# Routed FFN behind graph attention: four banks for each engine in the node loop, root node ahead of the sort, final stores that add to an output that holds x

## The chip, the cores and the metric

One core of one Trainium2 chip runs the whole program. The metric is the device time of one execution in microseconds. The core's engines are TensorE (PE, matrix products into PSUM), VectorE (DVE), ScalarE (ACT), GpSimd (POOL) and SyncE (SP, which here only issues DMAs). The kernel uses PSUM as eight banks of 128 partitions by 512 f32 values.

## The reference

```python
x = x + gnn(layernorm(x), neigh, adj, ...)        # x: 512 x 128, adj: 512 x 512, 8 heads
h = layernorm(x)
current = 0                                       # each token starts at the root of a tree, 255 nodes
for level in range(8):
    score = h . w1s[current] + b1s[current]
    out  += gelu(|score|) * (h @ w2s[current] + b2s[current])
    current = 2 * current + 1 + (score > 0)
return x + out
```

Every token goes down a binary tree. At each of its eight nodes it is multiplied by that node's own 128 x 128 matrix. Node 0, the root, is on the path of every token.

## The kernel before

The first part (up to about 61 us) is the attention: scores, softmax and weighted values for 4 tiles of 128 tokens and 8 heads. Then x1 = x + attention is made (512 x 128, in `x1`), normalised, turned (`h_t`), and scored against all 255 nodes at once. DVE makes `path`, a 0/1 row of nodes per token. The tokens are then sorted by their leaf: a permutation matrix `perm` sorts, on PE, the paths (L745 into `s_ps`), the weights (L745 into `aux_ps`) and the tokens themselves (L784, `hs_t` after ACT's copy L522). In a sorted tile of 128 tokens only few nodes occur. They are written out as one list per tile, `nodes` (PE L791, ACT L524), made up to a multiple of 8 entries with a node that has coefficient 0. `coef` holds, for each sorted token and node, gelu(|score|) or 0 (DVE L1094), and its transpose `coef_t` serves for the biases b2 (PE L563, ACT L531).

The node loop is what runs last. Every turn takes 8 list entries of one sorted tile. PE multiplies the tile's tokens by the eight node matrices (L820), product j into bank j: `s_ps` holds banks 0 to 3, `turn_ps` 4 and 5, `aux_ps` 6, `misc_ps` 7. DVE takes banks 0, 2, 3, 5, 7: it multiplies by the node's column of `coef` and adds to one of three sums in `acc` (an early name of that room is `early`, and so it stands in the profile), all in one instruction (L1115). ACT takes banks 1, 4, 6: it scales into `scaled_sb` (L542), and POOL adds that to one of two more sums (L401). A bank is free for the next turn when its consumer is done (`emptied`). All four engines run the same loop (`tile_turns`, a hardware loop per tile with a turn count from the list's length), and each has to read the list entries into registers: PE eight at the head of a turn (L97), DVE and ACT eight in the middle of it (L85). L90 is the address worked out from such a register, L118 the loop.

After a tile's turns PE makes the bias products (L830) and ACT moves them (L549). DVE sums the six partial sums of a tile in one reduction (L1130), for tiles 0 and 1 after tile 1, for tile 2 after tile 2, for tile 3 at the end. x1 itself comes in by a detour: it is written in token order to `x1_rows` in HBM (ACT L491), gathered from there by the sorted token numbers into the first sum (POOL L384), and the summed tile is scattered to the output by the same numbers (POOL L409).

The reference's inputs give the four sorted tiles 31, 24, 17 and 48 nodes that occur, root included, and so 4, 3, 3 and 6 turns, 16 together.

## Time and profile before

| | us |
|---|---|
| median of 3 runs | 137.24 |
| lowest, highest | 135.8, 138.54 |
| the profiled execution | 134.76 |
| its span in the profile | 133.0 |
| busy PE / DVE / ACT / POOL | 107.4 / 96.7 / 66.0 / 38.7 |
| TensorE's granted clock, mean of the span | 0.985 of full |

The span runs from the first to the last instruction of the trace, and the profiled execution's own time is 1.76 us more. The sections of the profile used here are the chain that ended last, the groups of instructions by line, and the timeline, in which every row is an instruction or a run of like ones, with its start, its length, its engine and line, what it writes and reads, and in brackets how long the engine sat idle before it and for whom.

### The profile page before, as it was taken

The numbers are of one execution on the slowest core, as the hardware profiler recorded it, in microseconds if no ns is written. First come the engines' busy times: TensorE is split into PE (matmuls) and PEld (weight loads), VectorE is DVE, ScalarE is ACT, GpSimd is POOL, SyncE is SP. The second block draws the span as 40 slices with busy tenths as digits, with TensorE's granted clock in tenths as the row PEclk, the third lists the DMA queues.
The fourth block names the chain that finished last, engine by engine and source line by source line (L and its number), as shares of the span: only waits on it lengthen the run. The fifth ranks groups of instructions, "written<-read, shape, count | busy, mean of one in ns | idle before, by whom it ended". The sixth has DMA issues, their size and how long they took to land.

```text
span 133.0 us, 3457 instructions
## 1 busy us (share of the span) xinstructions
PE 107.4 (81%) x984; PEld 76.2 (57%) x985; DVE 96.7 (73%) x293; ACT 66.0 (50%) x149; POOL 38.7 (29%) x84
## 2 busy tenths in 40 slices
PE   6989889559999999988998679989888499678800
PEld 2349663335656566657564353788778388578700
DVE  1787799988989989825888995367455976856760
ACT  3047288549777967931191644634344233344300
POOL 6394000000000000000400023155566436855552
PEclk9999999999999999999999999999999999999995
DMA  3998899989992000029992001000000000100000
GB/s 96 324 312 273 374 463 473 424 362 463 463 419 103 2 0 5 0 68 378 386 412 82 1 0 44 0 0 0 20 2 0 22 0 2 39 0 0 0 20 20
DMA packets 3420, 20.14 MB, mean 151 GB/s; under 512 B 465, under 2 KB 2000, under 8 KB 2896
## 3 DMA queue, kind: packets, MB, share of 16 engines
q1 hardware_dynamic: 2048, 18.42, 34.2%
q10 hardware_dynamic: 1104, 1.05, 2.5%
q0 software_dynamic: 256, 0.52, 1.4%
q8 instruction: 6, 0.10, 0.3%
q14 instruction: 6, 0.05, 0.1%
HBM read 19.47 MB, written 0.52 MB: 150 GB/s over the span
## 4 chain that ended last, share of the span: by engine, by line
PE 33%; DVE 19%; issue 10%; DVEq 10%; ACT 7%; POOL 1%
PE turn_ps L674 9%; DVE early L1115 6%; DVEq L90 4%; PE s_ps L820 4%; DVEq L85 4%; PE s_ps L620 3%; ACT prob L474 3%; DVE x L1130 2%; PE misc_ps L639 2%; DVE token_path L1034 2%; PE turn_ps L820 1%; PE s_ps L707 1%; PE s_ps L559 1%; PE turn_ps L563 1%; ACT prob_t L470 1%
## 5 line engine op out<-in xcount | busy, mean ns | idle before, releaser
L401 POOL TENSOR_TENSOR early<-early,scaled_sb 128x128 f32<-128x128 f32 x48 | 21.1, 455 | 20.0 <-ACT scaled_sb L542 18.4
L820 PE MATMUL s_ps<-w,msg 128*128 x128 | 18.8, 287 | 7.5 <-issue 3.6
L474 ACT ACTIVATE prob<-prob,negmax 128x512 f32<-128x512 f32 x32 | 21.7, 715 | 6.1 <-DVE negmax L994 6.1
L994 DVE CUSTOM_DVE_ANT_0 prob<-s_ps,mask 128x512 f32<-128x512 f32 x32 | 21.0, 685 | 3.3 <-PE s_ps L620 2.6
L674 PE MATMUL turn_ps<-ident,prob 128*128 128x128 f32 x128 | 19.2, 283 | 3.7 <-ACT prob L474 3.7
L820 PEld LDWEIGHTS s_ps<-w,msg 128*128 128x128 f32 x128 | 15.6, 191 | 10.5 <-issue 10.3
L1115 DVE SCALAR_TENSOR_TENSOR early<-s_ps,coef,early 128x128 f32<-128x128 f32 x48 | 14.2, 346 | 7.6 <-PE s_ps L820 4.3
L674 PEld LDWEIGHTS turn_ps<-ident,prob 128*128 128x128 f32 x128 | 13.6, 141 | 10.5 <-ACT prob L474 10.1
L373 POOL TENSOR_TENSOR rstd<-veps,mhalf 128x2 f32<-128x2 f32 x2 | 1.4, 714 | 52.4 <-DVE veps L854 52.4
L542 ACT ACTIVATE scaled_sb<-s_ps,coef 128x128 f32<-128x128 f32 x16 | 5.9, 368 | 14.6 <-PE s_ps L820 13.1
L1115 DVE SCALAR_TENSOR_TENSOR early<-turn_ps,coef,early 128x128 f32<-128x128 f32 x16 | 5.6, 350 | 9.2 <-issue 8.5
L542 ACT ACTIVATE scaled_sb<-turn_ps,coef 128x128 f32<-128x128 f32 x16 | 5.9, 367 | 9.4 <-PE turn_ps L820 9.4
L820 PE MATMUL turn_ps<-w,msg 128*128 x64 | 9.9, 277 | 0.0
L620 PE MATMUL s_ps<-early 32*128 32x512 bf16 x96 | 7.4, 377 | 2.2 <-DVE negmax L994 1.9
L1003 DVE COPY w<-turn_ps 128x512 f32<-128x512 f32 x12 | 8.3, 690 | 0.8 <-PE turn_ps L674 0.7
L470 ACT ACTIVATE w<-turn_ps 128x512 f32<-128x512 f32 x12 | 7.1, 592 | 3.4 <-PE turn_ps L674 2.8
L820 PEld LDWEIGHTS turn_ps<-w,msg 128*128 128x128 f32 x64 | 8.4, 192 | 0.1
L559 PE MATMUL s_ps<-count_row,ones_h 128*128 128x512 f16 x33 | 8.4, 379 | 0.0
L384 POOL DMA_INDIRECT early<-x_rows,token_s x4 | 4.1, 1026 | 14.3 <-ACT token_s L519 13.6
L1130 DVE TENSOR_REDUCE x<-early 128x128 f32<-128x768 f32 x4 | 5.8, 1463 | 1.1 <-DVE early L1115 1.1
L579 PE MATMUL s_ps<-early 128*128 128x512 bf16 x12 | 5.2, 624 | 1.3 <-DVE early L880 1.3
L820 PE MATMUL aux_ps<-w,msg 128*128 x32 | 6.2, 275 | 0.0
(189 smaller groups left out, 196.2 us busy)
## 6 DMA issues: line engine op xcount, KB each, us to landing
w<-in_w_t SPq DMA_DIRECT2D x3, 4096.0 KB, 22.9
w<-in_w_t SPq DMA_DIRECT2D x1, 4032.0 KB, 14.2
w<-in_adj SPq DMA_DIRECT2D x1, 1024.0 KB, 8.4
w_sb<-in_w_t ACTq DMA_DIRECT2D x1, 384.0 KB, 4.4
x_sb<-in_x SPq DMA_DIRECT2D x1, 256.0 KB, 3.2
msg<-in_neigh_t SPq DMA_DIRECT2D x1, 256.0 KB, 4.0
x_rows<-x ACTq DMA_DIRECT2D x1, 256.0 KB, 10.2
row_sb<-in_rows ACTq DMA_DIRECT2D x1, 255.5 KB, 7.7
```

The costliest lines, as they stand in the source:

```text
L401: nc.gpsimd.tensor_tensor(mine, mine, scaled_sb[:, i, :], ALU.add).then_inc(pooled[i], STEP)
L470: nc.scalar.activation(slots[v % SLOTS], turn_ps[0][:], ACT.Copy).then_inc(moved[0], 1)
L474: nc.scalar.activation(prob[:, u % RING, :], prob[:, u % RING, :], ACT.Exp, bias=negmax[:, t, h:h + 1], scale=-1.0).then_inc(exped, 1)
L542: nc.scalar.activation(scaled_sb[:, i, :], product_ps[j], ACT.Copy, scale=coef[:, s, bass.ds(node_at(nc.scalar, entry, j), 1)]).then_inc(s ...
L559: nc.tensor.matmul(s_ps[:, 3, :], ones_h[:], count_row[:], start=True, stop=True)
L620: ins = nc.tensor.matmul(score_ps[u % RING], q_st[rows, q, g, t * P:(t + 1) * P], k_st[rows, k, g, :], start=(i == 0), stop=(i == len(PROD ...
L674: last = nc.tensor.transpose(turn_ps[u % 2][:, m * P:(m + 1) * P], prob[:, u % RING, m * P:(m + 1) * P], ident[:])
L820: nc.tensor.matmul(product_ps[j], hs_t[:, s * P:(s + 1) * P], w2_flat[:, bass.ds(found[j], D)], start=True, stop=True).then_inc(multiplied ...
L994: nc.vector.tensor_tensor_reduce(out=prob[:, u % RING, :], in0=score_ps[u % RING], in1=mask[:, t, :], scale=1.0, scalar=0.5 * MASKED, op0= ...
L1003: nc.vector.tensor_copy(slots[v % SLOTS], turn_ps[1][:]).then_inc(moved[1], 1)
L1115: nc.vector.scalar_tensor_tensor(out=mine, in0=product_ps[j], scalar=coef[:, s, bass.ds(node_at(nc.vector, entry, j), 1)], in1=mine, op0=A ...
L1130: nc.vector.tensor_reduce(result[:, tile, :], acc[:, :, tile, :].rearrange("p j d -> p d j"), AX_X, ALU.add).then_inc(tile_done, 1)
```

## The change

- **Banks.** DVE takes banks 1, 3, 5, 7 with two sums and ACT takes banks 0, 2, 4, 6. POOL adds two scaled products in one instruction of 128 x 256, two such a turn in place of three of 128 x 128. DVE and ACT read only their own four entries, at the head of a turn.
- **Root.** It is left out of the sort's lists. Behind the node scores PE multiplies `h_t` by the root's matrix, unsorted, and ACT scales it (`root_sb`). The lists then hold 30, 23, 16 and 47 nodes, and so 4, 3, 2 and 6 turns.
- **Output.** `x1_rows`, its store and the four gathers go. POOL adds `root_sb` to `x1`, SP stores that to `out` in token order, and each sorted tile is then added to `out` by a scatter whose DMA adds.
- **Sums.** The reductions L1130 go. After tiles 0, 1 and 2 POOL itself adds up four sums in two instructions (three for tile 0, which has its bias apart), and issues the scatter. Only the last tile's are added by DVE.
- **First turn.** The first turn stands ahead of the loop and ahead of the transposes of `coef`. The list is made in two halves, and the sorting of the tokens in two halves around that of the weights. Nine fillers (`keep_busy`) stand where 13 did, and the four ahead of the loop go.

On PE, between the sort of the paths and the node loop, the instructions stood in this order (`w` is the node matrices, `msg` the sorted tokens, `prob` the permutation and the chosen lists):

```order
L745 MATMUL s_ps<-token_path,prob 128x256 x15
L745 MATMUL aux_ps<-picked_p,prob 128x24 [waits counts_moved,picked_split]
L784 MATMUL turn_ps<-prob,h_p 128x512 x7
L791 MATMUL s_ps<-prob,node_col 1x512 [waits chosen_ready]
L791 MATMUL s_ps<-prob,node_col 1x512 x3
L559 MATMUL s_ps<-count_row,ones_h 128x512 [waits path_s_ready]
L105 TENSOR_LOAD entries [waits w2_in3,b2_in,w2_in2,lengths_ready,w2_in1,w2_in0]
L563 MATMUL turn_ps<-ident,coef 128x128 [waits coef_ready,hs_ready,lists_ready]
L563 MATMUL misc_ps<-ident,coef 128x128 x4
L97 TENSOR_LOAD row_room
L820 MATMUL s_ps<-w,msg 128x128
```

and stand now in this one:

```order
L810 MATMUL s_ps<-token_path,prob 128x256 x15
L844 MATMUL s_ps<-prob,node_col 1x512 [waits chosen_ready]
L853 MATMUL turn_ps<-prob,h_p 128x512 x3
L810 MATMUL aux_ps<-picked_p,prob 128x24 [waits counts_moved,picked_split]
L853 MATMUL turn_ps<-prob,h_p 128x512 x4
L844 MATMUL s_ps<-prob,node_col 1x512 [waits chosen_ready]
L98 TENSOR_LOAD row_room [waits lists_ready,weights_added,path_s_ready]
L890 ISA [waits scaled0,hs_ready]
L890 MATMUL s_ps<-w,msg 128x128
L890 MATMUL misc_ps<-w,msg 128x128
L617 MATMUL s_ps<-ident,coef 128x128 [waits scaled0,coef_ready]
L617 MATMUL s_ps<-ident,coef 128x128 [waits scaled1]
```

The first eight node products no longer wait for `coef`, and its transposes stand behind them. Half of the list and half of the sorted tokens come ahead of the weights' sort.

On POOL one tile's loop and what follows it was, for the first tile (the scatters came later):

```order
L401 TENSOR_TENSOR early<-early,scaled_sb 128x128 [waits pooled2,scaled0]
L401 TENSOR_TENSOR early<-early,scaled_sb 128x128 [waits scaled1]
L401 TENSOR_TENSOR early<-early,scaled_sb 128x128 [waits pooled0,scaled2]
L118 COMPARE_AND_BRANCH
L384 DMA early<-x_rows,token_s 128x128
```

and is now:

```order
L419 TENSOR_TENSOR early<-early,scaled_sb 128x2x128 [waits scaled1,pooled1,scaled0]
L419 TENSOR_TENSOR early<-early,scaled_sb 128x2x128 [waits scaled3,pooled0,scaled2]
L123 REGISTER_ALU x3
L123 COMPARE_AND_BRANCH
L425 REGISTER_ALU x2
L429 TENSOR_TENSOR early<-early 128x2x128 [waits added3,added2,pooled1]
L433 TENSOR_TENSOR x<-early 128x128 [waits x1_out,result_ready]
L439 TENSOR_TENSOR x<-x,early 128x128 [waits bias_moved,result_ready]
L444 DMA out_x<-x,token_s 512x128 [waits tile_done]
```

Each add of a pair waits for the one before it, and the tile's own sums stand in POOL's queue ahead of the next tile's adds.

On DVE one turn, from the loop's head to its end, was

```order
L90 ISA [waits added3,multiplied0]
L1115 SCALAR_TENSOR_TENSOR early<-s_ps,coef,early 128x128
L90 ISA [waits added4,multiplied2]
L90 ISA [waits multiplied3]
L85 TENSOR_LOAD row_room
L1113 REGISTER_ALU [waits multiplied5]
L1115 SCALAR_TENSOR_TENSOR early<-turn_ps,coef,early 128x128
L90 ISA [waits added1,multiplied7]
L1115 SCALAR_TENSOR_TENSOR early<-misc_ps,coef,early 128x128
L118 COMPARE_AND_BRANCH
```

and is now

```order
L123 ISA
L85 TENSOR_LOAD row_room
L90 ISA [waits added2,multiplied1]
L1193 SCALAR_TENSOR_TENSOR early<-s_ps,coef,early 128x128
L90 ISA [waits added3,multiplied3]
L1191 REGISTER_ALU [waits multiplied5]
L1193 SCALAR_TENSOR_TENSOR early<-turn_ps,coef,early 128x128
L90 ISA [waits added1,multiplied7]
L1193 SCALAR_TENSOR_TENSOR early<-misc_ps,coef,early 128x128
L123 REGISTER_ALU x3
L123 COMPARE_AND_BRANCH
```

One instruction on a bank is gone, the load of the entries moved from the middle to the head, and three register operations stand at the loop's end. The core of the diff:

```diff
-DVE_BANKS = (0, 2, 3, 5, 7)
-ACT_BANKS = (1, 4, 6)
-DVE_SUMS = 3
+HALVES = 1
+TURN = HALVES * STEP
+DVE_BANKS = (1, 3, 5, 7)
+ACT_BANKS = (0, 2, 4, 6)
+DVE_SUMS = 2
...
     start = STEP
+    whole_turn(0, STEP, 0)
+    begun()
     for s in range(TILES):
...
+        with eng.Fori(start + TURN if s == 0 else start, end, TURN) as e:
+            whole_turn(s, e, e - start + s * NODES_PAD)
         after(s, end)
...
+            sp.wait_ge(root_added, 1)
+            sp.dma_start(out.rearrange("(t p) d -> p t d", p=P), x1[:]).then_inc(x1_out, 16)
...
+            pool.wait_ge(coef_ready, 2)
+            nc.gpsimd.tensor_tensor(x1[:], x1[:], root_sb[:], ALU.add).then_inc(root_added, 1)
+
+            def add_scaled(s, half, e, at):
+                for i in range(len(pooled)):
+                    pool.wait_ge(scaled[2 * i], e + STEP)
+                    pool.wait_ge(scaled[2 * i + 1], e + STEP)
+                    pool.wait_ge(pooled[1 - i], e + (HALVES - 1 + i) * STEP)
+                    mine = acc[:, DVE_SUMS:SUMS, s, :]
+                    slot = half * len(ACT_BANKS) + 2 * i
+                    nc.gpsimd.tensor_tensor(mine, mine, scaled_sb[:, slot:slot + 2, :], ALU.add
+                                            ).then_inc(pooled[i], STEP)
...
+                nc.gpsimd.indirect_dma_start(out=out, out_offset=bass.IndirectOffsetOnAxis(
+                    ap=token_s[:, s:s + 1], axis=0), in_=result[:, s, :], in_offset=None, compute_op=ALU.add
+                                             ).then_inc(stored, 16)
...
+            for t in range(TILES):
+                nc.scalar.activation(root_sb[:, t, :], turn_ps[1][:, t * P:(t + 1) * P], ACT.Copy,
+                                     scale=root_w[:, t:t + 1]).then_inc(root_scaled, 1)
...
-            keep_busy(13)
+            for t in range(TILES):
+                nc.tensor.matmul(misc_ps[:, t:t + 1], ones_row[:], row_sb[0:1, B1:B1 + 1], start=True, stop=False)
+                last = nc.tensor.matmul(misc_ps[:, t:t + 1], h_t[:, t * P:(t + 1) * P], w1_sb[:, 0:1],
+                                        start=False, stop=True)
+            last.then_inc(root_scored, 1)
+            pe.wait_ge(w2_in[0], 16)
+            for t in range(TILES):
+                last = nc.tensor.matmul(turn_ps[1][:, t * P:(t + 1) * P], h_t[:, t * P:(t + 1) * P], w2[:, 0, :],
+                                        start=True, stop=True)
+            last.then_inc(root_scored, 1)
+
+
+            keep_busy(9)
...
             def sum_up(s, end):
+                if s == TILES - 1:
+                    for i in range(DVE_SUMS, len(DVE_BANKS)):
+                        dve.wait_ge(added[i], end)
+                    dve.wait_ge(pooled[1], end + (HALVES - 1) * STEP)
+                    mine = acc[:, 0:DVE_SUMS, s, :]
+                    then(nc.vector.tensor_tensor(mine, mine, acc[:, DVE_SUMS:SUMS, s, :], ALU.add))
+                    nc.vector.tensor_tensor(result[:, s, :], acc[:, 0, s, :], acc[:, 1, s, :], ALU.add
+                                            ).then_inc(tile_done, 1)
```

## Rows read from the trace of the kernel before

**Rows 1.** Chain that ended last, one piece of tile 3 (start us, us, what).

```profile
118.99 0.35 DVEq L85
```

**Rows 2.** Timeline, two turns of tile 3: DVE alone.

```profile
117.18 0.35 DVE L1115 SCALAR_TENSOR_TENSOR early<-turn_ps,coef,early 128x128 f32<-128x128 f32 x1 [0.66 <-issue]
...
118.11 0.88 DVE L1115 SCALAR_TENSOR_TENSOR early<-s_ps,coef,early 128x128 f32<-128x128 f32 x3 [0.31 <-issue]
119.65 0.35 DVE L1115 SCALAR_TENSOR_TENSOR early<-turn_ps,coef,early 128x128 f32<-128x128 f32 x1 [0.66 <-issue]
```

**Rows 3.** Timeline, third and fourth turn of tile 0: PE, ACT, POOL.

```profile
88.95 1.15 PE L820 MATMUL s_ps<-w,msg 128*128 x8 [0.25 <-issue]
...
89.82 0.37 ACT L542 ACTIVATE scaled_sb<-s_ps,coef 128x128 f32<-128x128 f32 x1 [0.79 <-PE s_ps L820]
...
90.32 0.46 POOL L401 TENSOR_TENSOR early<-early,scaled_sb 128x128 f32<-128x128 f32 x1 [0.54 <-ACT scaled_sb L542]
...
90.96 0.36 ACT L542 ACTIVATE scaled_sb<-aux_ps,coef 128x128 f32<-128x128 f32 x1
...
91.15 1.15 PE L820 MATMUL s_ps<-w,msg 128*128 x8 [0.15 <-issue]
```

**Rows 4.** Timeline: what stands between tiles, and the end.

```profile
93.03 1.06 PE L830 MATMUL s_ps<-b_sb,prob_t 128*128 128x128 f32 x8
...
103.15 2.86 DVE L1130 TENSOR_REDUCE x<-early 128x128 f32<-128x768 f32 x2 [0.63 <-DVE early L1115]
...
115.97 0.45 POOL L401 TENSOR_TENSOR early<-early,scaled_sb 128x128 f32<-128x128 f32 x1 [0.17 <-POOL early L401]
...
127.91 1.45 DVE L1130 TENSOR_REDUCE x<-early 128x128 f32<-128x768 f32 x1 [0.24 <-DVE early L1115]
129.63 0.96 POOL L409 DMA_INDIRECT out_x<-x,token_s  x1 [1.02 <-DVE x L1130]
```

**Rows 5.** Timeline ahead of the node loop.

```profile
67.96 2.97 PE L559 MATMUL s_ps<-count_row,ones_h 128*128 128x512 f16 x13
...
71.40 0.25 PE L725 MATMUL aux_ps<-ones_h,token_path 128*128 128x1 f16 x4 [0.47 <-DVE token_path L1034]
...
78.59 0.56 PE L745 MATMUL aux_ps<-picked_p,prob 128*128 128x24 bf16 x16 [0.81 <-DVE picked_p L867]
...
79.01 1.89 PE L784 MATMUL turn_ps<-prob,h_p 128*128 128x512 f16 x8
...
80.11 1.70 DVE L1094 TENSOR_TENSOR coef<-token_path_s,weight_s 128x4 f32<-128x4 f16 x8
...
80.83 1.02 PE L791 MATMUL s_ps<-prob,node_col 128*1 128x512 f16 x4
...
80.93 0.60 ACT L522 ACTIVATE msg<-turn_ps 128x512 f32<-128x512 f32 x1 [2.03 <-PE turn_ps L784]
...
81.89 1.01 ACT L524 ACTIVATE row_room<-s_ps 1x1024 int32<-1x1024 f32 x1 [0.36 <-PE s_ps L791]
...
83.96 1.15 PE L820 MATMUL s_ps<-w,msg 128*128 x8
```

**Rows 6.** Timeline around POOL's one wide add.

```profile
9.58 0.74 DVE L877 SCALAR_TENSOR_TENSOR w<-w,from_even 128x512 f32<-128x512 bf16 x1
9.66 1.80 POOL L368 TENSOR_TENSOR x_sb<-x_sb,row_sb 128x512 f32<-128x512 f32 x1
...
10.97 0.78 DVE L917 TENSOR_TENSOR early<-w,early 128x256 bf16<-128x256 f32 x1 [0.65 <-ACT early L448]
```

**Rows 7.** Groups of instructions by line, whole span, shapes apart.

```profile
L917 DVE TENSOR_TENSOR early<-w,early 128x768 bf16<-128x768 f32 x1 | 0.9, 948 | 0.0
...
L1010 DVE TENSOR_TENSOR x<-x_sb,misc_ps 128x256 f32<-128x256 f32 x1 | 0.4, 422 | 1.3 <-PE misc_ps L702 1.3
```

**Rows 8.** DMA issues, median us from issue to landing.

```profile
early<-x_rows,token_s POOLq DMA_INDIRECT x4, 2.6
out_x<-x,token_s POOLq DMA_INDIRECT x4, 2.2
```

More of the change, by code:

```diff
@@ L105, in list_lengths, with tile_turns, whole_turn, gnn_ffn_kernel @@
     _, lengths = nc.values_load_multi_w_load_instructions(
-        entries[0:1, 0:TILES], engines=(engine,), min_val=STEP, max_val=NODES_PAD)
-    return lengths
-def tile_turns(eng, lengths, entry, nodes, turn, after):
+        entries[0:1, 0:TILES], engines=(engine,), min_val=TURN, max_val=NODES_PAD,
+        skip_runtime_bounds_check_because="lengths are counts of nodes turned up to at least one turn")
+    return lengths
+def tile_turns(eng, lengths, turn, begun, after):
+    def whole_turn(s, e, at):
+        for half in range(HALVES):
+            turn(s, half, e + half * STEP, at + half * STEP)
     start = STEP
+    whole_turn(0, STEP, 0)
+    begun()
     for s in range(TILES):
-        end = eng.snap(lengths[s] + start)
-        if entry is not None:
-            first_entries(eng, entry, nodes, s)
-        with eng.Fori(start, end, STEP) as e:
-            turn(s, e, e - start + s * NODES_PAD)
+        end = eng.snap((lengths[s] & (2 * NODES_PAD - TURN)) + start)
+        with eng.Fori(start + TURN if s == 0 else start, end, TURN) as e:
+            whole_turn(s, e, e - start + s * NODES_PAD)
         after(s, end)
         start = end
-def gnn_ffn_kernel(nc, x, adj, neigh_t, w_t, cols, rows, w1_t, w2_t, b2, x1_rows, out):
+def gnn_ffn_kernel(nc, x, adj, neigh_t, w_t, cols, rows, w1_t, w2_t, b2, out):
     with ExitStack() as ctx:
@@ L403, in store @@
-            def store(s, end):
-                if s < GROUPS[0][1]:
-                    gather(s + GROUPS[0][1])
-                for tile in STORED_AFTER[s]:
-                    pool.wait_ge(tile_done, tile + 1)
-                    nc.gpsimd.indirect_dma_start(out=out, out_offset=bass.IndirectOffsetOnAxis(
-                        ap=token_s[:, tile:tile + 1], axis=0), in_=result[:, tile, :], in_offset=None
-                                                 ).then_inc(stored, 16)
-            tile_turns(nc.gpsimd, list_lengths(nc, pool.engine, entries), None, nodes, add_scaled, store)
+            pool.wait_ge(acc_zero, SUMS)
@@ L772, in _, with lists, sorted_h @@
             last.then_inc(path_sorted, 1)
+            def lists(half):
+                pe.wait_ge(chosen_ready, 2 * (half + 1))
+                for c in range(2):
+                    last = nc.tensor.matmul(s_ps[0:1, half, :], node_col[:, c:c + 1],
+                                            chosen[:, c, half * 512:(half + 1) * 512],
+                                            start=(c == 0), stop=(c == 1))
+                last.then_inc(listed, 1)
+            def sorted_h(t0, t1):
+                for t in range(t0, t1):
+                    for i in range(2):
+                        last = nc.tensor.matmul(turn_ps[1][:], h_p[:, t, i, :], perm[:, t, :],
+                                                start=(t == 0 and i == 0), stop=(t == TILES - 1 and i == 1))
+                return last
+            lists(0)
+            pe.wait_ge(h_split, 2)
+            sorted_h(*GROUPS[0])
             pe.wait_ge(picked_split, 2 * PARTS - 1)
@@ L802, in _, with products @@
             lengths = list_lengths(nc, pe.engine, entries)
-            pe.wait_ge(lists_ready, 1)
-            pe.wait_ge(hs_ready, 1)
-            pe.wait_ge(coef_ready, 1)
-            for c in range(2):
-                transposes((turn_ps[1], misc_ps)[c], coef[:, :, c * P:(c + 1) * P], coef_turned)
+            pe.wait_ge(path_s_ready, 1)
+            pe.wait_ge(weights_added, 1)
+            pe.wait_ge(lists_ready, 2)
             w2_flat = w2[:].rearrange("p n o -> p (n o)")
-            def products(s, e, at):
+            def products(s, half, e, at):
```

275 lines of the change are left out of this document (147 added, 128 removed).

## Prediction

> **What bounds the kernel now.** Read the chain that ended last first, since a mean of busy time hides where the end is set. From 95 us on it runs over DVE: its adds L1115, its register load L85 [rows 1] and its reductions L1130. The timeline of DVE alone shows why. A turn takes 119.65 - 117.18 = 2.47 us [rows 2]: three adds 0.27 apart (0.88 in all), 0.66 idle while eight entries are loaded, two adds, and 0.31 idle at the loop's end. Add up to see that nothing else is in it: 0.88 + 0.66 + 0.62 + 0.31 = 2.47. PE alone is faster: in tile 0, where it runs ahead, its turns are 91.15 - 88.95 = 2.20 us apart [rows 3]. So DVE sets the pace of the loop, and between tiles it stops for the reductions, 2.86 + 1.45 us inside the loop and 1.45 at the end [rows 4]. The node loop begins at 83.96 [rows 5] and the last sum is ready at 127.91 + 1.45 = 129.36, which leaves 133.0 - 129.36 = 3.64 us for the scatter.
>
> **The change, part by part.** I place each turn by the start of its first product, T1 to T15, and build a new timeline in the time of the profiled span (133.0).
>
> *Root ahead of the sort.* PE runs 13 fillers in 2.97 us and then sits idle 0.47 for the path [rows 5]. Four fillers go (4 x 0.214 = 0.86). New are four products of 128 x 128 in f32, eight passes of 0.11 as in the loop (16 passes in about 1.76) = 0.88, and eight of one column, 16 passes. Those are not in the trace. Below they cost 0.035 each (the 16 narrow ones of the weights' sort, 0.56), above 0.11 each (1.76). I take 0.06, nearer the narrow rows, since one column streams nothing and only the f32 load is left: 0.96. Net 0.88 + 0.96 - 0.86 = 0.98, less the 0.47 of idle: PE is 0.5 late, with ends 0.1 and 1.3. As the fillers may overlap a little with that I take **+0.4**, and everything behind moves by it, since DVE waits there for PE's count. ACT's new work (two small, four of 128 x 128) fits its idle time before it needs the scores.
>
> *First turn sooner.* PE waited 0.81 for the weights' split at 78.59 [rows 5]. Half of the list (half of 1.02) and half of the tokens (half of 1.89) now fill that. The sort of the paths frees PE at about 77.6, so the order ends at 77.6 + 0.47 + 0.92 + 0.56 + 0.92 + 0.47 = 80.95. ACT copies the tokens (0.60) from 80.7 and then the list's second half (0.55 of 1.01), to 81.9, where it ended at 82.90. With the register load of some 0.45, T1 = 82.4 against 83.96. `coef` (until 81.81) no longer bounds PE. DVE's and ACT's first instructions wait for it and for their loads until about 83.0, when the first product is just out. The eight transposes (0.9) follow the first turn: T2 = 82.4 + 1.78 + 0.9 + 0.42 = 85.5, against 86.65 before. Cover gone would show as T2 later by ACT's two copies of 0.60.
>
> *Banks.* DVE's turn is now 3 x 0.27 + 0.35 = 1.16 of adds, plus 0.66 and 0.31 if load and loop end stand one behind the other: 2.13, and some 0.1 for three register operations. ACT's is the same. PE needs 2.20 and gets the same register operations. I take **2.25** a turn for all three, PE being the bound by a hair. One turn of 16 is gone. T3 to T15 are 13 x 2.25, and two bias blocks of 0.9 [rows 4] stand between: without further waits T15 = 85.5 + 29.25 + 1.8 = 116.55.
>
> *POOL.* The new question is its add of 128 x 256. The 128 x 128 one takes 0.46 [rows 3], the only wide one, 128 x 512, took 1.80 [rows 6]. A straight line through both gives 0.90. But that wide one started under a DVE instruction with two SBUF inputs that ended at 10.32, and the DVE instruction after it, again with two SBUF inputs, took 0.78 us for 256 columns [rows 6], where the same form with 768 took 0.95 [rows 7]: each held the other up. Taken from 10.32, POOL's ran 1.14 us, a slope of 1.8 ns a column, and 128 x 256 costs 0.46 + 128 x 0.0018 = 0.69. DVE's adds in the loop have one SBUF input (the other is PSUM), and POOL's 0.46 there does not waver. I take 0.70. The Trainium skill, "SBUF — State Buffer", section "Who interferes with whom", says the same as a rule: a DVE instruction with two SBUF inputs contends with a GpSimd one that reads SBUF, and the later one waits. By that rule 0.70 stands and the forecast is 130.7. By the plain line of the rows (0.90) it would be 134.6, as the rival below works out.
>
> A turn on POOL is then 2 x 0.70 + 0.17 (the wait for its own last add over the loop's end [rows 4]) + 0.05 for the same wait inside the turn, a guess that no row bounds from above but the 0.17, = 1.62 < 2.25. Behind a tile stand its sums and the scatter: 0.70 + 2 x 0.46 + 0.96 [rows 3, 4] and some 0.6 of waits between them (0.17 each) = 3.2 for tile 0, 2.7 for tiles 1 and 2 with one add less. ACT's last scaling starts 2.0 after T (90.96 - 88.95), so a turn's pairs end at T + 2.0 + 0.37 + 0.13 + 0.70 = T + 3.2 and start at T + 1.6. A first pair that is late by L frees ACT's room at T + 2.3 + L and PE's bank at T + 2.85 + L, which PE wants two turns on, at T + 4.5: L up to 1.65 costs nothing. After tile 0, L = 3.2 + 3.2 - (2.25 + 0.9 + 1.6) = 1.65. Each turn after a tile's first wins back 2.25 - 1.62 = 0.63, so tile 1 ends with L = 0.4, and tile 2 begins with 3.2 + 0.4 + 2.7 - 4.75 = 1.55. Tile 2 has two turns and no bias block: L = 3.2 + 0.9 + 2.7 - (2.25 + 1.6) = 2.95, which is 1.3 over the 1.65 that is free, a stall of **1.3**. T15 = 117.85, and POOL's last add ends at 121.1.
>
> *The end.* DVE's two adds (0.42 [rows 7], some 0.3, waits 0.1) replace 0.24 + 1.45: 121.9. Then the same 3.64 as before: 125.5. The scatter now adds. No row shows one. Below it costs nothing more; above, one more trip like the gather's, 2.6 us [rows 8], in place of part of the 2.2. I take **0.5**, since it moves the same 512 bytes a row and only its read of HBM is new. The Trainium skill, "DMA: Bandwidth & Descriptors", section "Rules for kernel authors", states that an accumulating DMA reads its destination and writes it later, and prices neither. That reading in full is a rival below. The store of x1 by SP (after the weights, its queue is empty) starts near 83.5 and is wanted near 94, so it is hidden; late, it would hold POOL at tile 0. The removed gathers and the removed store of x1 were off the path.
>
> Sum: 125.5 + 0.5 + 0.4 = 126.4, and 126.5 unrounded, a gain of 6.5 on 133.0. The profiled execution (134.76) lies below all three runs shown, so I set the gain against their median: 137.24 - 6.5 = **130.7**.
>
> **The rivals.**
> 1. *POOL becomes the bound* (its wide add takes 0.90). Then POOL never rests from tile 0 on. From T4 = 90.0 its last add ends at 90.0 + 3.6 + 3.4 + 2.9 + 2.9 + 11 x 2.02 = 125.0 in place of 121.1: 134.6. For it: the raw row of 1.80. Against: the DVE row of 0.78.
> 2. *The load at the head costs what it cost in the middle, and more*: DVE and ACT take 2.45 a turn. 13 x 0.20 = 2.6: 133.3. For it: load, loop end and register operations now stand in one string with no product to hide behind. Against: the branch back is issued while the last adds run, so that part of the 0.31 falls away.
> 3. *The scatter reads first, a whole trip*: + 2.1, 132.8. For it: the rule named above. Against: only the last scatter is on the path.
> 4. *The other side: the adding scatter is dear on POOL itself.* If its issue takes X more than 0.96, the three inside the loop delay POOL by 3X and the last the end by X. POOL has 121.1 - 119.6 = 1.5 in hand over the whole loop (90.0 + 3.2 + 3.2 + 2.7 + 2.7 + 11 x 1.62 = 119.6), so the end moves by 4X - 1.5. It is slower than before by 2% (140.0) from X = 2.7, and at X = 3, so 4 us a scatter, it gives 141.2. For it: nothing shown. Against: the gather and the plain scatter, both near 1.0.
> 5. *No change within 2%*: rival 1 and the root's upper price (1.3 in place of 0.4) together, 134.6 + 0.9 = 135.5.
>
> **How the numbers follow.** Forecast 0.55, rival 1 0.13, rival 2 0.12, rival 3 0.11, rival 4 0.05, rival 5 0.04. Below, with no stall, no cost of the adding scatter and none of the root, it is 128.5, and 1 us of spread between runs makes 127.5. Above, rivals 1 to 3 lie inside 135.0. Two per cent is about what a measurement of this kernel can tell, that is below 134.5 for faster. Half of rival 1 falls above it, with rival 5 and part of rival 2: faster 0.80, same 0.14, slower 0.06.
>
> **What would show it.** Right: PE's turns 2.2 to 2.3 us apart; L419 on POOL near 0.70 each; first product about 1.2 us sooner; no DVE reduction in the loop; 15 turns; one wait of PE near the second turn of the last tile, traced back to POOL. Wrong: POOL busy without a gap from tile 1 on (rival 1), DVE with over 1.2 us idle a turn on "issue" (rival 2), over 4.5 us from the last DVE add to the end (rival 3), scatters over 2 us on POOL (rival 4). TensorE's clock stays at 9 tenths in the page through the waits at the tiles' ends today, and the new ones are no longer; a fall to the lower level would be an error of mine.

## The result and the profile after

The changed kernel takes 138.32 us (median of 4, 137.76 to 139.5), the kernel before 136.52 beside it on the same chip (135.33 to 138.54): a ratio of 1.022 [1.016, 1.028], so slower by 1.6 to 2.8%. The forecast was 130.7. The profiled span is 136.0 us, against 133.0 before and 126.5 in the sum.

Executions of one and the same kernel differ by how often TensorE's granted clock falls to its lower level: the 23 of the kernel before that stood beside the last experiments run from 134.5 us at a mean granted clock of 0.985 over 136.4 at 0.963 to 138.2 at 0.951, so the ratios here leave out executions over 1.5% above the fastest of their kernel, and I judge the steps of the sum by stretches of the traces whose clock is known.

The first row of clocks is that of the profile after, 40 equal slices of 3.4 us. It falls at 29 to 33 us, in a part that the change does not touch, and again near 105:

```profile
PEclk9999999977999999999999999999998699999985
```

The timeline at the root's products (start us, us, engine, line; PE's work and the first instruction of DVE behind it):

```profile
68.93 0.38 PE L776 MATMUL misc_ps<-row_sb,ones_row 1*128 1x1 f32 x2
69.24 0.38 PE L777 MATMUL misc_ps<-w_sb,h_t 128*128 128x1 f32 x2
...
71.34 1.14 PE L782 MATMUL turn_ps<-w,h_t 128*128 128x128 f32 x8
72.32 2.11 PE L613 MATMUL s_ps<-count_row,ones_h 128*128 128x512 f16 x9
74.26 0.24 PE L790 MATMUL aux_ps<-ones_h,token_path 128*128 128x1 f16 x4
...
74.54 0.29 DVE L1119 CAST leaf_count<-aux_ps 128x128 f16<-128x128 f32 x1 [2.32 <-PE aux_ps L790]
```

Eight groups of one column stand 0.31 us apart, 68.93 to 71.34: 2.4 us where the sum had 0.96. PE was idle for 0.47 before its leaf count in [rows 5]; now it is late, and DVE waits 2.32 for that count (0.35 in the kernel before).

The first turns (ACT's last copy of the list, and PE's first product of each turn):

```profile
84.03 0.59 ACT L566 ACTIVATE row_room<-s_ps 1x512 int32<-1x512 f32 x1
...
85.71 1.15 PE L890 MATMUL s_ps<-w,msg 128*128 x8 [1.72 <-issue]
...
89.06 1.20 PE L890 MATMUL s_ps<-w,msg 128*128 x8 [0.43 <-ACT prob_t L593]
...
91.73 1.15 PE L890 MATMUL s_ps<-w,msg 128*128 x8 [0.58 <-issue]
...
94.26 1.15 PE L890 MATMUL s_ps<-w,msg 128*128 x8 [0.49 <-issue]
```

From the end of the list (84.62) to the first product are 1.09 us, and the turns of tile 0 are 2.67 and 2.53 apart, where [rows 3] has 2.20 and the sum 2.25. The sequencer's records say what PE is doing in those 0.58 and 0.49 us (count, then ns least/median/most):

```profile
L123 PEldq ALU_OP  x43: 32/36/43, 90.2 to 128.5; - x43
...
L123 PEldq COMPARE_BRANCH  x14: 76/208/243, 90.5 to 128.6; - x14
...
L98 PEldq TENSOR_LOAD <-row_room x15: 588/592/776, 84.8 to 126.7; - x15
```

(PEldq is the part of PE that works through registers, waits and branches.) Three register operations a turn stand at the loop's end where the kernel before has one (L122 computes the end with a mask), then the branch, and then the load of eight entries, 0.59 us. The load for the third turn starts at 90.88, as late as the last product of the second.

POOL at the end of tile 0, and what PE waits for then; the groups of POOL's adds and scatters; and the clock by stretches (us; busy time and instructions of each engine; granted clock):

```profile
97.66 0.72 POOL L429 TENSOR_TENSOR early<-early 128x256 f32<-128x256 f32 x1
...
100.78 1.74 POOL L444 DMA_INDIRECT out_x<-x,token_s  x1 [1.32 <-issue]
102.03 1.25 POOL L419 TENSOR_TENSOR early<-early,scaled_sb 128x256 f32<-128x256 f32 x1
103.45 0.72 POOL L419 TENSOR_TENSOR early<-early,scaled_sb 128x256 f32<-128x256 f32 x1 [0.17 <-POOL early L419]
...
104.01 1.96 PE L890 MATMUL s_ps<-w,msg 128*128 x8 [2.03 <-ACT scaled_sb L585]
```

```profile
L419 POOL TENSOR_TENSOR early<-early,scaled_sb 128x256 f32<-128x256 f32 x30 | 23.4, 780 | 11.6 <-ACT scaled_sb L585 8.6
...
L444 POOL DMA_INDIRECT out_x<-x,token_s x4 | 6.4, 1595 | 3.0 <-issue 1.3
```

```profile
100.00:104.00 4.00, 1.98 (x16) 1.79 (x16) 1.26 (x4) 0.49 (x2) 3.06 (x3) 1.00 0.19 18
104.00:108.00 4.00, 3.99 (x21) 4.00 (x22) 1.18 (x4) 2.12 (x7) 2.35 (x4) 0.57 0.00 0
```

The adds cost what was forecast, 0.72 (the mean of 0.78 comes from those right behind a scatter, 1.25 to 1.30). The adding scatter costs POOL 1.54 to 1.74 in place of 0.96 [rows 4], lands after 3.3 us in place of 2.2 [rows 8], and slows the next add. PE waits 2.03 us, and its clock then falls to 0.57, so that eight passes take 1.96 us in place of 1.15. ACT waits for POOL for 11.9 us in all. The second such wait, 1.80 at 120.03, is followed by no fall; the kernel before had waits of 1.89 and 1.15 in its loop (106.40 and 114.23), and no fall either.

### The profile page after: what moved, and what is told of

Read it like the earlier page. It is cut to its first block, busy times and chain, and to the rows that moved or that the text cites. A ratio compares the mean times of both kernels' runs of the same rounds, so it can differ in the third digit from the quotient of the medians.

```text
span 136.0 us, 3475 instructions
## 1 busy us (share of the span) xinstructions
PE 108.9 (80%) x984; PEld 79.6 (59%) x985; DVE 88.6 (65%) x272; ACT 71.6 (53%) x169; POOL 43.1 (32%) x70
## 4 chain that ended last, share of the span: by engine, by line
PE 46%; issue 9%; POOL 9%; ACT 8%; DVE 5%; ACTq 1%; POOLq 1%; DVEq 0%
PE turn_ps L728 10%; PE s_ps L890 8%; POOL early L419 6%; PE s_ps L674 3%; PE s_ps L613 3%; PE turn_ps L890 3%; ACT prob L509 2%; PE misc_ps L693 2%; PE aux_ps L693 2%; ACT scaled_sb L585 2%; PE s_ps L761 1%; PE s_ps L810 1%; PE turn_ps L853 1%; ACT prob_t L505 1%; PE aux_ps L890 1%
## 5 line engine op out<-in xcount | busy, mean ns | idle before, releaser
L419 POOL TENSOR_TENSOR early<-early,scaled_sb 128x256 f32<-128x256 f32 x30 | 23.4, 780 | 11.6 <-ACT scaled_sb L585 8.6
L890 PE MATMUL s_ps<-w,msg 128*128 x120 | 18.1, 296 | 10.6 <-ACT scaled_sb L585 5.2
L1193 DVE SCALAR_TENSOR_TENSOR early<-s_ps,coef,early 128x128 f32<-128x128 f32 x30 | 10.3, 351 | 21.2 <-PE s_ps L890 20.2
L728 PE MATMUL turn_ps<-ident,prob 128*128 128x128 f32 x128 | 20.1, 295 | 3.4 <-ACT prob L509 3.4
L728 PEld LDWEIGHTS turn_ps<-ident,prob 128*128 128x128 f32 x128 | 14.6, 148 | 10.1 <-ACT prob L509 9.3
L585 ACT ACTIVATE scaled_sb<-s_ps,coef 128x128 f32<-128x128 f32 x30 | 10.1, 365 | 18.6 <-POOL early L419 11.1
L444 POOL DMA_INDIRECT out_x<-x,token_s x4 | 6.4, 1595 | 3.0 <-issue 1.3
L410 POOL TENSOR_TENSOR x<-x,root_sb 128x512 f32<-128x512 f32 x1 | 1.3, 1262 | 18.7 <-DVE coef L1171 18.7
L613 PE MATMUL s_ps<-count_row,ones_h 128*128 128x512 f16 x25 | 6.5, 380 | 0.0
L890 PE MATMUL misc_ps<-w,msg 128*128 x30 | 6.1, 285 | 0.0
```

The lines of the kernel that those rows point to most:

```text
L419: nc.gpsimd.tensor_tensor(mine, mine, scaled_sb[:, slot:slot + 2, :], ALU.add).then_inc(pooled[i], STEP)
L444: nc.gpsimd.indirect_dma_start(out=out, out_offset=bass.IndirectOffsetOnAxis(ap=token_s[:, s:s + 1], axis=0), in_=result[:, s, :], in_offs ...
L585: nc.scalar.activation(scaled_sb[:, half * len(ACT_BANKS) + i, :], product_ps[j], ACT.Copy, scale=coef[:, s, bass.ds(node_at(nc.scalar, en ...
L613: nc.tensor.matmul(s_ps[:, 3, :], ones_h[:], count_row[:], start=True, stop=True)
L728: last = nc.tensor.transpose(turn_ps[u % 2][:, m * P:(m + 1) * P], prob[:, u % RING, m * P:(m + 1) * P], ident[:])
L890: nc.tensor.matmul(product_ps[j], hs_t[:, s * P:(s + 1) * P], w2_flat[:, bass.ds(found[LISTED_AT[j]], D)], start=True, stop=True).then_inc ...
```

## The experiments

I compare two stretches: the **head**, from the two sides' first row on DVE to the first product of the first turn (after: 68.25 to 85.71 = 17.46), and the **loop**, from there to the first product of the fifteenth turn (after: 127.42 - 85.71 = 41.71).

### The changed kernel without the fillers

```
-            keep_busy(9)
```

> The changed kernel without its nine fillers between the root's products and the leaf count; all else is the same. In the changed kernel PE comes to the leaf count at 74.26 us and DVE has waited 2.32 us for it, where the path was ready about 72.2. Theory (the root's eight one-column products, 0.31 us each, make PE late, and the nine fillers of 0.214 behind them lie on the path): DVE's wait falls from 2.32 to about 0.5, the first node product comes 1.8 us sooner and the time falls by 1.5 to 2.0 us. Rival A (ACT's root work and its four zeroings, which end at 75.8, are what holds the sort): the wait falls but the first node product comes less than 1 us sooner, since ACT's sums of the deep levels then start late. Rival B (the fillers keep the granted clock up): the clock of the stretch 68 to 85 falls under 0.9 and the gain is lost.

138.24 us, 1.020 [0.989, 1.051]. DVE's wait for the leaf count shrinks from 2.32 to 1.35 and the head by 0.7, where about 0.5 and 1.8 were expected. But in this trace the clock fell at 66 us, ahead of the root's products, and again at 73 us, and in that of after it did neither, so its head and its time settle nothing.

Its loop, which the edit does not touch, is of use. The clock stays up there through a wait as long as that of after:

```profile
105.17 1.15 PE L889 MATMUL s_ps<-w,msg 128*128 x8 [2.19 <-ACT scaled_sb L585]
```

The loop is 41.31 us, against 41.71 with the fall: by these two executions the fall behind the wait cost the loop of after some 0.4 us, and the waits are there without it.

### The changed kernel with scatters that store

```
-  in_=result[:, s, :], in_offset=None, compute_op=ALU.add
+  in_=result[:, s, :], in_offset=None
```

> The changed kernel with its four scatters as plain stores: they no longer add to what the output holds, so x and the root's part are left out of the result. Theory (the adding scatter is what is dear on POOL: 1.54 to 1.74 us of issue each against 0.98 of the plain one before): each L444 falls to about 1.0, POOL comes 0.6 us sooner to the next tile after each of three tiles, PE's waits of 2.03 us after tile 0 and 1.80 in tile 3 shrink to about 1.3, the end (4.4 us from DVE's last sum) shrinks to 3.7, together 1.5 to 3 us less, more if the clock's fall at 104 us goes too. Rival (it is POOL's own sums and its waits, not the adding): L444 stays at 1.5 or the loop does not move, under 0.7 us less.

136.48 us, 1.017 [1.002, 1.032]. The group of scatters, and tile 1's first add and PE's wait:

```profile
L444 POOL DMA_INDIRECT out_x<-x,token_s x4 | 4.1, 1037 | 3.1 <-issue 1.4 <-DVE x L1204 1.2 <-ACT scaled_sb L585 0.3
```

```profile
102.06 0.73 POOL L419 TENSOR_TENSOR early<-early,scaled_sb 128x256 f32<-128x256 f32 x1
...
103.52 1.15 PE L890 MATMUL s_ps<-w,msg 128*128 x8 [1.58 <-ACT scaled_sb L585]
```

The add starts as late as before but takes 0.73 in place of 1.25, PE waits 1.58 instead of 2.03, the clock stays up, and the loop is 39.55 us: 2.16 less than after, and 1.76 less than the loop of the run above, in which the clock stays up too. From DVE's last add to the end it is 3.33 in place of 4.4. So the adding scatter costs up to 3.3 us of this trace (136.0 against 132.7), some 0.4 of it through the clock, and 1.8 by the medians.

### The changed kernel with the tiles' sums on DVE, one tile late

```
+ STORED_AFTER = ((), (0,), (1,), (2, 3))
...
-   if s < TILES - 1:
-       pool.wait_ge(pooled[1], end + (HALVES - 1) * STEP)
...
+   for tile in STORED_AFTER[s]:
+       pool.wait_ge(tile_done, tile + 1)
```

> The changed kernel with the sums of a tile taken from POOL and given to DVE, one tile late (tile 0 after tile 1's turns, tile 1 after tile 2's, tiles 2 and 3 at the end), with the scatter as late on POOL. DVE idles over 20 us in the loop, POOL's tail behind a tile falls from 4.4 us after tile 0 (and about 3.8 after tiles 1 and 2) to one scatter of about 1.6. Theory (POOL's sums stand ahead of the next tile's adds, hold ACT's room and so PE's banks): the waits of ACT for POOL of 3.9 and 3.3 us go to under 1, PE's waits of 2.03 and 1.80 go, the clock no longer falls to 0.57 at 104 to 108, and the time falls by 4 to 6 us in spite of about 1 us more at the end for the second scatter there. Rival (the loop is slow because of the head of each turn, 2.5 to 2.7 us between turns already in tile 0 where POOL is idle): the loop falls by under 2 us.

136.66 us, 1.013 [1.000, 1.026]. The loop is 37.35 us, 4.4 less than after, and ACT waits for POOL for 5.8 in place of 11.9. The gain does not reach the median whole (1.7 less than after): in this trace the clock fell at 72 to 76 us and DVE waited 4.01 for the leaf count, and the end, with two tiles' sums and two scatters behind the last turn, is 1.6 longer.

### The kernel before, with scatters that add to a stored x1

```
-  dma_start(x1_rows.rearrange(...), x1[:])
+  dma_start(out.rearrange(...), x1[:])
-  gather(t)
...
+  compute_op=ALU.add
```

> The kernel before with one part of the change alone: x1 is stored to the output, the four gathers go, one more sum is zeroed by ACT, and the four final scatters add. Theory: the gathers were off the path, the two scatters in tile 3 delay POOL by 0.6 us each, which DVE's slower turn hides, and only the last scatter counts: +0.5 to +1.0 us at the end, 3.64 us from the last sum to the end becoming 4.3 to 4.5. Rival (scatter's adding is dear everywhere): +2 us or more. Rival (the gathers held POOL and the loop): faster than before by 1 us or more.

136.6 us, 1.017 [1.005, 1.029]. The loop is as before (40.23 for 40.19, 16 turns); scatters take 1.54 to 1.74 here too. From the last sum (130.42) to the end (134.7) are 4.3 us in place of 3.64. Away from a full POOL, the adding scatter costs 0.65, near the 0.5 of the sum. The ratio alone would speak for the rival of 2 us or more. But 1.07 us of this trace's 1.7 lie ahead of the sides (68.44 for 67.37), behind a fall of the clock at 25 us, and where the kernel before has a like mean clock (0.962 to 0.964) it takes 135.8 to 136.8 us, this one 136.45 and 136.7 at 0.959.

### The changed kernel without the mask at the loop's end

```
-  end = eng.snap((lengths[s] & (2 * NODES_PAD - TURN)) + start)
+  end = eng.snap(lengths[s] + start)
```

> The changed kernel with the loop's end as before: the length is added to the start without the mask, and its bounds are asserted once when the lengths are loaded. That takes three register operations and one branch operand off the end of every turn on every engine. In the changed kernel PE's sequencer works through three register operations (0.1 us each from start to start) and then starts the load of the eight entries (0.59 us) about when the last product starts, where before it started it 0.4 us sooner; PE then idles 0.49 to 0.67 us a turn in tiles 0 to 2 against 0.15 to 0.25. Theory (this is what the turn lost): the turns of tile 0 come 2.25 to 2.35 us apart in place of 2.67 and 2.53, and the time falls by 1.5 to 3 us. Rival (the turn is held by ACT and POOL, not by PE's sequencer): the spacing in tile 0 stays over 2.5 and the time falls by under 0.7 us.

The lengths' bounds are stated once, where they are loaded. 138.06 us (fastest 136.40, where the changed kernel's is 137.76), 1.011 [1.003, 1.018]; in the profiled execution, of 139.19, the clock fell three times ahead of the loop, at 29, 67 and 74 us. In the loop it did not, and tile 0 reads:

```profile
92.92 1.19 PE L889 MATMUL s_ps<-w,msg 128*128 x8 [0.43 <-ACT prob_t L592]
95.43 1.15 PE L889 MATMUL s_ps<-w,msg 128*128 x8 [0.42 <-issue]
97.69 1.15 PE L889 MATMUL s_ps<-w,msg 128*128 x8 [0.22 <-issue]
...
121.99 1.15 PE L889 MATMUL s_ps<-w,msg 128*128 x8 [2.00 <-ACT scaled_sb L584]
```

Turns of 2.51 and 2.26 in place of 2.67 and 2.53, and a loop of 39.27: 2.4 less than after, 2.0 less than the loop without a fall (41.31). The waits for POOL are still there (2.00).

### The changed kernel with the transposes ahead of the first turn

```
-    whole_turn(0, STEP, 0)
     begun()
+    whole_turn(0, STEP, 0)
...
- TURNED_IN = (0, 2)
+ TURNED_IN = (5, 7)
```

> The changed kernel with the transposes of coef ahead of the first turn, as before the change, in banks 5 and 7. In the changed kernel the lists are ready at 84.62 us and coef at 84.63, so the first turn had nothing to run ahead of: its register load stands bare (1.09 us from the lists to the first product, where before it lay under the transposes), and the second turn waits for ACT's copies of the transposes (T2 is 3.35 us after T1, before 2.69). Theory (first turn ahead is no gain, or a loss): from the lists' end to the second turn's first product 4.44 us now, 3.75 before; this kernel gives about 3.8 to 4.0, and the time falls by 0.3 to 0.8 us. Rival (the first turn ahead does save the transposes' time): the second turn comes later by 0.5 us or more.

137.1 us, 1.014 [1.007, 1.022]. ACT's list ends at 86.81 here:

```profile
87.97 1.13 PE L890 MATMUL s_ps<-w,msg 128*128 x8
...
90.47 1.15 PE L890 MATMUL s_ps<-w,msg 128*128 x8 [0.48 <-issue]
```

3.66 us from the list's end to the second turn, where after has 89.06 - 84.62 = 4.44. The first turn had gained no lead in which the transposes could hide; behind it they were only in the second's way. The next turns gain as well, with the mask still in place:

```profile
92.78 1.15 PE L890 MATMUL s_ps<-w,msg 128*128 x8 [0.26 <-issue]
...
95.08 1.15 PE L890 MATMUL s_ps<-w,msg 128*128 x8 [0.26 <-issue]
```

2.31 and 2.30 us in place of 2.67 and 2.53. In after every turn of tile 0's loop also has to pass two waits for ACT's copies of the transposes (`coef_t_ready`), and each takes PE's sequencer some 0.1 us though from the third turn on the copies are long there; in this kernel they stand in the first turn alone.

### The changed kernel with the root's scores copied from the nodes' scores

```
-   nc.tensor.matmul(misc_ps[:, t:t + 1], ones_row[:], ...)
-   last = nc.tensor.matmul(misc_ps[:, t:t + 1], h_t[...], w1_sb[:, 0:1], ...)
...
+   nc.vector.tensor_copy(root_w[:], node_scores[:, :, 0]).then_inc(root_scored, 1)
```

> The changed kernel with the root's scores taken from the node scores that are there already (one small DVE copy behind the path) in place of the eight one-column products, and ACT's four zeroings ahead of the root's weights. The fillers stay at nine. Theory (the one-column products, 0.31 us each, are what makes PE 2 us late at the leaf count): DVE's wait for the leaf count falls from 2.32 us to 0.35 or a little more, the first node product comes 1.9 us sooner counted from the node scores, and the time falls by 1.5 to 2 us. Rival (ACT then becomes late, its root work now behind the path): the wait moves to the weights' split and under 1 us is won.

137.2 us, 1.010 [1.001, 1.019]. The root's score was already in the product of the two sides, and the copy costs DVE 0.15. (ACT's four zeroings also move ahead of its work on the root.) The rows:

```profile
71.19 0.15 DVE L1112 COPY root_w<-s_ps 128x4 f32<-128x4 f32 x1
71.62 0.29 DVE L1114 CAST leaf_count<-aux_ps 128x128 f16<-128x128 f32 x1 [0.27 <-PE aux_ps L784]
...
82.69 1.15 PE L884 MATMUL s_ps<-w,msg 128*128 x8 [1.63 <-ACT row_room L565]
...
101.22 1.95 PE L884 MATMUL s_ps<-w,msg 128*128 x8 [2.16 <-ACT scaled_sb L584]
```

The head is 82.69 - 67.30 = 15.39, 2.07 less than after, and the first product comes at 82.69, where the sum had it (82.4, or 82.8 with its price of the root). The loop keeps all its waits and its fall of the clock, 42.31.

### Three edits together: no mask, copied scores, sums on DVE

> Three repairs at once on the changed kernel: no mask at the loop's end, root scores from the node scores, and the tiles' sums on DVE a tile late. If the three causes are apart and add up: root 1.9, loop end 0.3 a turn for 12 turns less what POOL's waits hide (2 to 3), tile sums 3 to 4 less the second scatter at the end: 6 to 8 us less than the changed kernel, a span of 128 to 130 us without a fall of the clock, about 131 of time, which is faster than the kernel before by 3 to 5%. If they overlap (the same idle time counted twice, a slower POOL behind a faster PE): 133 to 135, the same as before.

131.06 us, 0.969 [0.964, 0.973]: faster than both kernels. That it comes near the forecast of 130.7 does not bear the forecast out, since it is another arrangement of the sums, the root's scores and the loop's end.

```profile
82.84 1.18 PE L866 MATMUL s_ps<-w,msg 128*128 x8 [1.64 <-issue]
86.22 1.19 PE L866 MATMUL s_ps<-w,msg 128*128 x8 [0.43 <-ACT prob_t L574]
88.75 1.15 PE L866 MATMUL s_ps<-w,msg 128*128 x8 [0.44 <-issue]
...
119.18 1.15 PE L866 MATMUL s_ps<-w,msg 128*128 x8
...
125.23 1.54 POOL L426 DMA_INDIRECT out_x<-x,token_s  x1 [0.30 <-issue]
```

Head 15.41, loop 36.34, no fall of the clock before the end. The price is at the end: DVE sums two tiles and POOL issues two scatters behind the last turn, 10.1 us from the fifteenth turn's first product to the end where after has 8.6.

### The same, each edit taken back, and one added

The last four runs stood on one chip and the three edits on another; the kernel before was as fast on both (134.47 and 134.54 at its fastest). The first of the four adds the order of the transposes; each of the others takes one of the three edits back (that of the root with ACT's order).

> The kernel of r8 (no mask at the loop's end, root scores from the node scores, tile sums on DVE a tile late), and in addition the transposes of the coefficients stand ahead of the first turn instead of behind it, on two banks of their own. In r6 the same edit moved the way from the end of the lists (ACT L566, the old numbering) to the second turn's sum from 4.44 to 3.66 us. Theory (the first turn gained no lead, so it only puts the transposes between itself and the second turn): 0.7 to 0.8 us less than r8, some 130.3 us, with T2 about 5.7 us behind... the span at 128.5. Rival (the head is not what the later turns wait for, POOL or the tail takes the gain back): the same time as r8, with the 0.8 us found as a longer wait in the first tile.

> The kernel of r8 with the tile sums back on POOL, as in the changed kernel (no mask, root scores from the node scores). From the fifteenth sum minus the first in r8 (36.3 us) and in r5, which has POOL's sums and no mask (39.3): theory (POOL's two adds a turn plus its sum and a scatter of 1.5 us are what the loop waits for at a tile's end) 3 us more than r8, some 134 us, with PE idle for 1.3 to 2.2 us twice behind ACT, and ACT waiting for POOL 8 to 12 us in all. Rival (the loss in r5's and the changed kernel's loops came mostly from a fallen clock): within 1 us of r8 if the clock stays up.

> The kernel of r8 with the mask back at the loop's end (two more register operations a turn on each engine). Theory (they are bare on PE at the end of each turn): 0.15 to 0.25 us in the turns behind which nothing else is waited for; r3, masked and with the sums on DVE, had 37.35 us from the first sum to the fifteenth where r8 had 36.34, so 1.0 us more than r8, some 132 us. Theory at full strength (two operations of 0.1 us in each of 14 turns): 2.4 us more, 133.5 us. Rival (they lie under work): no more than 0.3 us.

> The kernel of r8 with the eight one-column products of the root's score back. Theory (they are 2.4 us bare on PE, and DVE's leaf counts wait for what is behind them): from the start of the product of the two sides to the first turn's sum 17.5 us where r8 has 15.4, and 2.1 us more in all, some 133.1 us; where TensorE's granted clock is at its lower level there, 3.5 us more. Rival (a shorter head is given back at the end of the loop): under 1 us more than r8.

| kernel | median us | fastest us | ratio to before | head | loop | span |
|---|---|---|---|---|---|---|
| three edits | 131.06 | 130.96 | 0.969 [0.964, 0.973] | 15.41 | 36.34 | 129.3 |
| and transposes first | 130.29 | 129.37 | 0.964 [0.955, 0.972] | 15.67 | 34.88 | 127.9 |
| sums on POOL again | 134.86 | 132.81 | 0.989 [0.982, 0.996] | 15.53 | 40.15 | 131.8 |
| mask again | 133.68 | 132.65 | 0.989 [0.981, 0.997] | 15.39 | 37.79 | 131.0 |
| root products again | 135.55 | 133.76 | 0.996 [0.990, 1.002] | 19.07 | 36.06 | 135.1 |

Each edit is worth something by itself: by the fastest executions 1.9 (sums), 1.7 (mask) and 2.8 us (root), 6.3 together, where the changed kernel's fastest of four (137.76) is 6.8 above the three edits'. By the medians of the executions that the ratios keep they are 2.5, 2.1 and 3.4; by the medians of all they are 3.8, 2.6 and 4.5, 10.9 together, more than the 7.3 between those two medians. The fastest executions differ least in how often the clock falls, but still differ (mean 0.987 for the three edits, 0.992 for the sums, 0.982 for the mask, 0.973 for the root, 0.959 for the changed kernel), so each size is known only to within these figures. The span of the last row is that of an execution of 136.86 us in which the clock fell at 29, at 66 and at 73 us.

With POOL's sums the loop is 3.8 us longer and the end 1.5 shorter, and the loop stops twice, though the clock is up at the first:

```profile
100.23 1.15 PE L883 MATMUL s_ps<-w,msg 128*128 x8 [1.42 <-ACT scaled_sb L583]
...
115.53 1.72 PE L883 MATMUL s_ps<-w,msg 128*128 x8 [1.97 <-ACT scaled_sb L583]
```

The rival of its expectation (all of it the clock) falls with the first of these rows. For the mask the truth lies between the middle theory (1.0 us) and full strength (2.4): 1.7 by the fastest executions and by the spans; the turns are 2.72 and 2.57 where the three edits have 2.53 and 2.32. For the root's products the theory's second case came out, 3.66 us in the head, since the clock fell right behind them (DVE's wait, and the stretch 73 to 76 us at half the clock). It had fallen at 66 us already, ahead of them:

```profile
77.75 0.29 DVE L1101 CAST leaf_count<-aux_ps 128x128 f16<-128x128 f32 x1 [3.97 <-PE aux_ps L772]
```

```profile
73.00:76.00 3.00, 3.00 (x12) 2.15 (x12) 0.75 (x2) 1.31 (x6) 0.00 (x0) 0.50 0.00 0
```

With the transposes first, the second and the next turns read:

```profile
85.37 1.15 PE L866 MATMUL s_ps<-w,msg 128*128 x8 [0.45 <-issue]
87.51 1.15 PE L866 MATMUL s_ps<-w,msg 128*128 x8
89.64 1.15 PE L866 MATMUL s_ps<-w,msg 128*128 x8
```

2.14 and 2.13 us a turn, PE without idle time: below the 2.20 of [rows 3]. The way from the third to the fourth turn, in four combinations, follows what PE's sequencer has to do: 2.13 without mask and waits, 2.30 with the mask (transposes first in the changed kernel), 2.32 with the waits (three edits), 2.57 with both (mask again). This is the best version, 0.8 below the three edits by the medians (the intervals of their ratios overlap).

## Why the prediction was wrong

The span came out 9.5 us above the sum (136.0 against 126.5). By its steps, in the order of time:

- **Upstream, +0.9.** The sides begin at 68.25 in place of 67.37, with a fall of the clock at 29 us: in the six traces without a fall there they begin between 67.2 and 67.5, in the eight with one at 68.25 or later. The instructions ahead of it are spaced the same, to a few hundredths of a us, in traces with the fall and without. It stands in all seven traces of kernels with the root's one-column products, which come 40 us later, and in one of the seven others; the kernel before, too, has executions at that mean clock. Whether this is chance stays open.
- **Root ahead of the sort, +2.0 in the head.** The step that failed is "I take 0.06, nearer the narrow rows". A pass of one column cost 0.155 us, above even the upper end of 0.11, and the term measured 2.07 (head 17.46 against 15.39) where the sum had 0.4 and its upper end 1.3. The narrow rows were bf16, in one group; these are f32 products in pairs. With the term taken out, the head is 15.39 where the sum has 82.4 - 67.37 = 15.03: the rest of "First turn sooner" was right to 0.36. That lies behind the end of the list: 1.00 us from there to the first product in that run where the sum had 0.5, the load of the registers at 0.59 and not 0.45, and 0.4 of waits and address that the sum left out.
- **Transposes, +0.25.** T2 - T1 was 3.35 for 3.1. That the order itself cost 0.8 (the first turn had no lead over them) is not in the prediction at all.
- **Banks, a turn of 2.53 to 2.67 in place of 2.25.** The step that failed is "some 0.1 for three register operations", together with the claim that PE is the bound "by a hair". The mask's operations, the branch and the 0.59 us load stand in one string on PE's sequencer, and the load stands behind the branch. Without the mask a turn is 2.26 to 2.5; the mask costs 1.5 us of the loop where nothing else is waited for (37.79 against 36.34), 2.0 to 2.4 in the changed kernel (41.31 or 41.71 against 39.27). In tile 0 the two waits for the transposes cost another 0.2 a turn, which the prediction does not have at all; without both a turn is 2.13. Rival 2 had this mechanism (2.45 a turn) on DVE and ACT; the trace has it on PE.
- **POOL.** Its add was right: 0.72 measured, 0.70 forecast, against 0.90 of the straight line. The rule of the Trainium skill, "SBUF — State Buffer", section "Who interferes with whom", by which 0.70 stood, agrees with this trace: the add of 128 x 256 takes 0.72 beside DVE's adds with one SBUF input, and a new one of 128 x 512, with no DVE instruction under it, 1.26 where the one of [rows 6] took 1.80 (the row below). Two guesses were not right: the wait between the two adds of a turn is 0.17 and not 0.05, a POOL turn 1.80 and not 1.62; and behind tile 0 POOL needs 4.4 us from its first sum to the next add (97.66 to 102.03), not 3.2, of which 1.32 is idle ahead of the first scatter. DMA transfers of instructions start at 98.79 and 100.71 there; whether they are the cause was not tried. The sum had the first turns behind tile 0 late by 1.65 us with 1.65 to spare, so the 1.2 us more went straight into a stall, and the one stall of 1.3 us became two, 2.03 and 1.80.

```profile
L410 POOL TENSOR_TENSOR x<-x,root_sb 128x512 f32<-128x512 f32 x1 | 1.3, 1262 | 18.7 <-DVE coef L1171 18.7
```

- **The adding scatter.** At the end its 0.5 was about right (0.65 measured in the kernel before). Inside the loop it was priced at nothing more than a plain one. It costs POOL 0.6 more itself and 0.5 in the next add; rival 4 described this, and by its formula X = 0.6 moves the end by 4 x 0.6 - 1.5 = 0.9 us. But the 1.5 of spare time was gone: 1.8 us of the loop hang on it with the clock up, 2.2 with the fall, and 1.0 at the end.
- **The clock.** "The new ones are no longer" was the error named in advance. The longest wait of the kernel before is 1.89 us, the new ones are 2.03 and 1.80, and the first was followed by a fall. It cost some 0.4 us of the loop (41.71 against 41.31), so the clock is a small part of the 6.0 below.

Loop and end together: from the second turn to the fifteenth 38.36 us in place of 32.35 (+6.0), and +0.3 behind it. Of the 6.0, 2.4 went with the mask and 2.2 with the adding scatter when each was taken away alone; moving the sums to DVE took away 4.4 alone (2.0, 1.8 and 4.0 against the loop without the fall). They overlap: the mask and the sums together took away 5.4 (41.71 against 36.34), where they are 6.8 one by one.

The outline of the gain holds: with four banks each, no DVE reductions and one turn less the kernel reaches 131.06 and 130.29, though with the sums as adds on DVE and not on POOL. How the gain divides among these parts was not tried. The sum failed on small guesses for operations that repeat 4 to 30 times: 0.06 for a pass, 0.05 for a wait, 0.1 for three register operations, nothing for a scatter inside the loop. The first two lay in the lower half of what their rows allowed, and the last two had no row.

## What to carry to other kernels

An operation that no trace shows should be priced at its upper end when it repeats in a loop, and a tiny matrix product is not a cheap one: eight products of one column (2.4 us) cost more than nine fillers (2.1). When an engine's slack is used up by two moved pieces of work, the third edit that is nearly free alone (here the adding scatter, 0.65 at the end and nothing in the loop) is paid in full, so the slack is to be recounted with all of them in. And before a value is computed again to be early, look whether it already lies in a result that is early.

## What the runs showed of the hardware

- f32 products of one column: 0.31 us for one product of two passes, 0.155 a pass, whatever the pass holds (sums over 1 row or over 128).
- In 5 of the 7 traces with these products the granted clock fell to its lower level (1.2 GHz) at 72 to 74 us, during or right behind them; in the 7 without them it never fell there. But in 3 of the 5 it had fallen at 66 to 67 us too, ahead of them, and all 7 have the fall at 25 to 29 us. Whether the products bring the later falls on was not tried.
- Behind a wait of PE of 1.97 to 2.19 us inside the loop the clock fell in four of six cases (after, copied scores, transposes first, sums on POOL), and did not in two (2.00, no mask; 2.19, no fillers); behind those of 1.26 to 1.92, the 1.89 of the kernel before among them, it did not.
- The adding indirect DMA: 1.54 us of POOL in place of 0.98, the first one of a kernel 1.74 (a plain one 1.20), and 1.25 to 1.30 for the 0.72 us add that starts under its tail.
- PE's sequencer: from one register operation, or wait that is met already, to the next some 0.1 us, a branch 0.2, a load of eight registers 0.59.
